# One transformer layer on one core: where the sums of three groups per pair of heads are added up, and where their row sums stand on TensorE

## The reference, cut to what matters

```python
def _L0_attn_ref(hidden_states, w_qkv, w_o):          # S = 2048 tokens, 16 heads of 32
    q, k, v = ...                                      # projections of the normalised x
    scores = jnp.einsum('bhqd,bhkd->bhqk', q, k) * scale
    scores = jnp.where(causal, scores, jnp.finfo(scores.dtype).min)
    probs = jax.nn.softmax(scores, axis=-1)
    attn = jnp.einsum('bhqk,bhkd->bhqd', probs, v)
    return jnp.einsum('bsh,oh->bso', attn, w_o)
...
    xn = _layernorm(x, axis=-1)
    x = x + _L0_attn_ref(xn, ...) + _L0_ffn_ref(xn, ...)   # the second is a gated MLP, 512 -> 4096 -> 512
```

## Time and profile before

| what | value |
|---|---|
| median of 3 runs | 1793.34 us (1793.21 to 1793.80) |
| the profiled execution's own time | 1794.05 us |
| its span | 1792.1 us |
| TensorE busy | 1753.0 us, 98% |
| VectorE busy | 1236.9 us, 69% |
| GpSimd busy | 752.8 us, 42% |
| ScalarE busy | 708.7 us, 40% |

### The profile page before, as it was taken

The page is one execution under the profiler, slowest core; times in us unless marked ns, Lnnn a source line. Parts: engine busy times, 40 slices in busy tenths (PEclk is TensorE's granted clock), DMA queues, the critical chain, the costliest instruction groups (busy, mean ns, idle before and its releaser), DMA issues.

```text
span 1792.1 us, 28186 instructions
## 1 busy us (share of the span) xinstructions
PE 1753.0 (98%) x10112; PEld 1340.7 (75%) x10112; DVE 1236.9 (69%) x1834; ACT 708.7 (40%) x1107; POOL 752.8 (42%) x716
## 2 busy tenths in 40 slices
PE   7999999999999998999999999999999999999998
PEld 6887666566566555888888888888888888888887
DVE  5526888888888888786566567567567666656654
ACT  3323666666666674223232223233223223222322
POOL 1442888988988985022212221222222212222221
PEclk9999999999999999999999999999999999999999
DMA  8775054154054011600110110110110011010002
GB/s 284 221 231 157 11 105 88 25 106 89 24 105 90 23 45 55 202 22 23 35 35 0 35 35 0 35 35 0 35 35 21 14 35 30 5 35 0 1 0 95
DMA packets 75614, 108.55 MB, mean 61 GB/s; under 512 B 24912, under 2 KB 44992, under 8 KB 72384
## 3 DMA queue, kind: packets, MB, share of 16 engines
q1 hardware_dynamic: 75520, 107.34, 22.1%
HBM read 74.04 MB, written 29.59 MB: 58 GB/s over the span
## 4 chain that ended last, share of the span: by engine, by line
PE 60%; DVE 0%; ACT 0%; issue 0%; ACTq 0%
PE p_up L50 7%; PE p_v L50 7%; PE p_up L52 7%; PE p_v L51 7%; PE p_up L51 7%; PE p_v L52 7%; PE p_s L50 6%; PE p_s L52 6%; PE p_s L51 6%; PE p_s L340 0%; PE p_s L339 0%; PE p_s L345 0%; PE p_v L339 0%; PE p_v L340 0%; PE p_up L340 0%; PE p_up L339 0%
## 5 line engine op out<-in xcount | busy, mean ns | idle before, releaser
L1418 POOL TENSOR_SCALAR poly<-poly 128x1024 f32<-128x1024 f32 (+1 forms) x65 | 72.0, 1108 | 801.4 <-ACT poly L1375 801.4
L753 POOL TENSOR_TENSOR e_sum<-e_sb 128x512 f32<-128x512 f32 (+1 forms) x244 | 304.1, 1271 | 62.2 <-ACT e_sb L839 33.7
L922 DVE TENSOR_REDUCE max_part<-p_s 128x1 f32<-128x512 f32 x384 | 246.4, 681 | 56.8 <-PE p_s L1033 56.5
L839 ACT ACTIVATE e_sb<-p_v 128x512 f32<-128x512 f32 (+2 forms) x384 | 212.6, 603 | 115.8 <-PE p_v L1064 60.4
L1481 DVE SCALAR_TENSOR_TENSOR inter<-inter,gate 128x1024 f32<-128x1024 f32 (+1 forms) x65 | 78.6, 1209 | 241.1 <-ACT inter L1381 240.3
L50 PE MATMUL p_v<-xn_hi,w_hi 128*128 128x512 f32 x512 | 199.2, 389 | 0.0
L51 PE MATMUL p_v<-xn_lo,w_hi 128*128 128x512 f32 x512 | 199.2, 389 | 0.0
L52 PE MATMUL p_v<-xn_hi,w_lo 128*128 128x512 f32 x512 | 199.2, 389 | 0.0
L50 PE MATMUL p_up<-xn_hi,w_hi 128*128 128x512 f32 x512 | 199.2, 389 | 0.0
L51 PE MATMUL p_up<-xn_lo,w_hi 128*128 128x512 f32 x512 | 199.2, 389 | 0.0
L52 PE MATMUL p_up<-xn_hi,w_lo 128*128 128x512 f32 x512 | 199.2, 389 | 0.0
(11 more groups left out here) (190 smaller groups left out, 3469.4 us busy)
## 6 DMA issues: line engine op xcount, KB each, us to landing
k_stack<-qk_scratch SPq DMA_DIRECT2D x42, 256.0 KB, 8.0
qk_scratch<-out_hi SPq DMA_DIRECT2D x32, 256.0 KB, 2.6
qk_scratch<-out_lo SPq DMA_DIRECT2D x32, 256.0 KB, 3.3
q_stack<-qk_scratch SPq DMA_DIRECT2D x24, 256.0 KB, 6.5
xn_lo_scratch<-xn_lo SPq DMA_DIRECT2D x4, 1024.0 KB, 5.2
v_stack<-in_gate_up_s SPq DMA_DIRECT2D x64, 64.0 KB, 2.3
xn_lo<-xn_lo_scratch SPq DMA_DIRECT2D x4, 1024.0 KB, 13.1
scales<-in_gate_up_s SPq DMA_DIRECT2D x64, 64.0 KB, 2.4
```

The costliest lines, as they stand in the source:

```text
L753: nc.gpsimd.tensor_tensor(*operands(k, i), ALU.add).then_inc(pool_summed, 1)
L839: nc.scalar.activation(e_sb[:, first:first + len(heads), 0:w], scores_of(x), ACT.Exp, scale=SCALE).then_inc(exp_done, 1)
L922: nc.vector.reduce_max(part, p_s[:, slot[n] % S_BUFS, 0:w], AX.X).then_inc(maxed, 1)
L1418: nc.gpsimd.tensor_scalar(part_of(poly, h, parts), part_of(poly, h, parts), GELU_A, 1.0, ALU.mult, ALU.add).then_inc(poly_done, 1)
```

## The change

`join_sums` of a group k is moved, if the group after it is diagonal and has all its 8 units: from ahead of unit 7 of its own group to amid the units of the diagonal group, ahead of unit 3, or of unit 4 where a turn of maxima stands in that group. These are groups 1, 4 and 8 of pairs 0 to 6, 21 in all (the last is 68). On TensorE the `row_sums` of the group ahead of a diagonal one is moved behind the four `product_v` of the diagonal group. This holds for all 24 such groups, those of the last pair too, where `join_sums` stays where it was.

```diff
+            def join_late(k):
+                return k + 1 < NG and DIAG[GS * (k + 1) % NS] and len(units_of(k + 1)) == UNITS_GROUP
...
                 for n in units:
-                    if n == units[-1]:
+
+
+                    if k and join_late(k - 1) and n == units[S_BUFS if TURNS[k] else S_BUFS - 1]:
+                        join_sums(k - 1)
+                    if n == units[-1] and not join_late(k):
                         join_sums(k)
                     unit_max(n)
...
-                if k and not DIAG[GS * (k - 1) % NS]:
+                diag = DIAG[GS * k % NS]
+                if k and not DIAG[GS * (k - 1) % NS] and not diag:
                     row_sums(k - 1)
                 for g in range(GS * k, GS * k + GS):
                     product_v(g)
+                if k and not DIAG[GS * (k - 1) % NS] and diag:
+                    row_sums(k - 1)
                 if DIAG[GS * k % NS]:
                     row_sums(k)
                 some_units(7, 8)
```

## The result

The change makes the kernel a little slower. The median of 13 runs is 1796.97 us (1796.01 to 1798.53), that of the kernel before, run between them, 1792.81 us (13 runs, 1791.77 to 1794.44): a ratio of 1.0023 [1.0016, 1.003], which is 4.2 us [2.9, 5.4]. The forecast was 1794.7. The profiled execution took 1796.14 us, with a span of 1794.2; that of before took 1794.05 with a span of 1792.1. In two comparisons further down one execution was far slower than all others (2143.64 us of the kernel before, 7479.17 us of split_first): the ratios leave it out, and the medians, which hold it, move by 0.2 us at most.

What follows compares the result with a forecast made beforehand. TensorE, busy for 98% of the span, bounds the kernel; only its waits in the attention can be won. Seven pairs +1.05, multiplies in three +0.9, last pair -0.6: +1.35 on 1793.34 gives 1794.7 us, range 1787 to 1802.

Steps and rivals of the forecast that it cites:

- the likeliest case: No change that the measurement can tell, within 0.2% (3.6 us), held by the forecast and D; chance 0.43.
- Group 12, -0.25 us: Without additions ahead of unit 7, TensorE's two waits shrink and the late additions run undisturbed: -0.25 us a pair.
- Groups 13 and 14, +0.65: GpSimd, held 2.3 us, puts a long sum beside `join_sums` of group 13, then 3.0 us: +0.65 us a pair.
- group 15, 0: VectorE's 1.37 idle us take the late additions, 1.33 us with GpSimd held: 0 for TensorE.
- Groups 16 to 18, +0.3 (+0.6): Late GpSimd lengthens `join_sums` of group 16, group 17's shortens: +0.3 us net, +0.6 in pairs 2, 4 and 6.
- 19, -0.55: In group 19 maxima and turn come 0.6 us earlier without the additions ahead: -0.55 us a pair.
- The last pair, -0.6: Group 79's products fill TensorE's idle time, row sum 1.16 us earlier; half taken lest the clock rise no earlier: -0.6.
- The sign named: A pair of heads taking 0.15 us more bears out the sum, 0.8 less A, 1.3 more B.
- A: Rival: GpSimd takes up its delays at `join_sums` of groups 13 and 16, gains stand alone: -6.2, 1787.1 us; chance 0.27.
- B: Rival: delays land in full at `join_sums` of group 16, group 19 gains only 0.2: +8.5, 1801.8 us; chance 0.22.
- C: Rival: row sums wait for 3.2 us additions in groups 12 and 15, 0.2 in 19: +13.4, 1806.7 us; chance 0.08.
- D: Rival: nothing hangs on it, waits for maxima pass to ScalarE's pace and back: 1793.3 us; chance 0.43 with the forecast.

Runs made afterwards that it cites:

- split_first: The changed kernel with GpSimd's split of the maxima ahead of its first two sums in groups 3, 13, ...: 1796.15 us, 1.0015 of the kernel before.
- late_1: The changed kernel with `join_sums` late only for groups 1, 11, ... 61: 1803.05 us, 1.005 of the kernel before.
- hold_only: The kernel before with the row sums moved and GpSimd held in groups 2, 12, ... 62 until VectorE's fifth unit is done: 1804.39 us, ratio 1.006.
- late_4: The changed kernel with `join_sums` late only for groups 4, 14, ... 64: 1793.83 us, 1.0004 of the kernel before.
- norm_later: The changed kernel with GpSimd's multiply moved from behind group 4 to behind group 5 in pairs 2, 4, 6 and the last: 1798.94 us, 1.003 of before.
- late_8: The changed kernel with `join_sums` late only for groups 8, 18, ... 68: 1789.86 us, 0.9984 of the kernel before.
- recip_late: The changed kernel with VectorE's reciprocal for the pair before moved from the group's head to ahead of unit 3: 1796.14 us, 1.0016 of the kernel before.
- late8_rows_before: The kernel before with `join_sums` late only for groups 8, 18, ... 68, row sums still ahead of the products: 1795.0 us, ratio 1.0007.
- late8_both: As late_8, with the reciprocal ahead of unit 3 and the last pair's multiply behind group 75: 1787.76 us, 0.9968 of the kernel before.
- late8_norm7: As late_8, with GpSimd's multiply behind group 74 (last pair alone) moved behind group 75: 1789.39 us, 0.9978 of the kernel before.
- rows_only: The kernel before with only TensorE's row sums moved behind the products, `join_sums` at its old place: 1793.03 us, ratio 0.9997.

## Why the prediction was right, and where it was off

The time came out 2.3 us above the forecast and inside the range. The range stated for the likeliest case, within 0.2%, was missed by a hair: +0.23% [0.16, 0.3], a little slower and not level. The mechanism is the forecast's: the late additions hold GpSimd, and `join_sums` of group 13 pays for it. Several sizes in it were not right, and they erred both ways; that the sum of them came out within 2.3 us is in part luck.

- *Group 12, -0.25 us.* Measured -0.20 in groups 12, 32, 42 and 62, and -0.14 in 22; 0.00 in group 2, which has no reciprocal. Together 7 x 0.25 = 1.75 was forecast, and the trace has 0.23, as one wait for the reciprocal's transfer takes 0.95 back.
- *Groups 13 and 14, +0.65, and group 15, 0.* Measured +0.60 to +0.65 in pairs 0, 1, 3 and 5. `join_sums` of group 13 takes 2.87 us where 3.0 was said, and GpSimd is held 2.3 us as said. That this size came out right is luck: by late_1 and hold_only the hold alone costs 1.1, and moving the additions of group 14, put at 0, gives 0.5 back.
- *The same in pairs 2, 4 and 6.* Here the step failed. "I take +0.65 us" was used for all seven pairs, and for group 15 "0 for TensorE" on the ground that GpSimd is held there. In these pairs GpSimd, late from the hold, is at its multiply (338.79) when the late additions come, and these take 2.49 us; by late_4, split_first and norm_later it takes both, the hold and the multiply. Measured +1.31, +1.58 and +1.30: 2.2 us more than forecast in sum, the largest part of the miss.
- *Groups 16 to 18, +0.3 (+0.6), and 19, -0.55.* Measured together -0.49 to -0.52 in the plain pairs, where -0.25 was said, and +0.05 in pairs 4 and 6, as said. Group 19 was right: late_8 gives -0.56 to -0.61 by itself. The +0.3 wasn't there: the additions of group 16 take 2.68 us in place of 1.84, those of group 17 2.82 in place of 3.20, and by late_1 and late_4 nothing of GpSimd's lateness is left over in TensorE's time (-0.02 and +0.05).
- *The last pair, -0.6.* Measured -1.15 at the row sums, which was the lower bound. I took half, lest the clock rise later. It did rise later: 706 to 712 is at the lower level, where before it was on its way up from 708 on (below). But from the row sums to the end of the span there are 1085.2 us in the change and 1085.9 before; over all 14 traces it is 1085.2 to 1086.7, whichever order they have. Nothing that can be told from that scatter was given back.

```profile
706.00:708.00 2.00, 0.46 (x8) 0.20 (x8) 1.85 (x4) 0.00 (x0) 0.00 (x0) 0.50 0.42 112
708.00:710.00 2.00, 1.60 (x20) 0.65 (x12) 1.84 (x5) 0.00 (x0) 0.00 (x0) 0.50 0.23 75
710.00:712.00 2.00, 2.00 (x9) 1.58 (x6) 2.00 (x4) 0.00 (x0) 0.00 (x0) 0.53 0.00 0
```

(The windows above are the changed kernel's; these are the same of the kernel before, whose second row sum came 2.8 us earlier in its trace.)

```profile
708.00:710.00 2.00, 2.00 (x9) 1.27 (x6) 1.41 (x1) 0.00 (x0) 0.00 (x0) 0.73 0.03 8
710.00:712.00 2.00, 2.00 (x10) 1.66 (x9) 1.87 (x5) 0.13 (x1) 0.00 (x0) 1.00 0.00 0
```

- *The sum.* From +1.35 to the trace's +3.3: +2.2 from pairs 2, 4 and 6, +1.5 from group 12 (its transfer, and pair 0), -1.0 from groups 16 to 19, and -0.55 from the last pair come to +3.5; -0.1 in groups 13 to 15 of the plain pairs and -0.1 in the pieces that were not to change make up the rest. The 0.9 us between these 3.3 and the 4.2 of the runs stay open. The transfer of the reciprocal may wait more often in other executions, which no trace shows; recip_late, which has no such wait, lies 2.8 us above the kernel before in place of 4.2, but that is not clear of the noise.
- *By pairs.* The sign named was a pair of heads that takes 0.15 us more, 0.8 less for A, 1.3 more for B. From one group 9 to the group 9 of the next pair, pairs 1 and 3 took 0.1 us less, pair 5 took 0.8 more with its wait for the reciprocal's transfer, and pairs 2, 4 and 6 took 1.1 to 1.4 more (the clock of before taken out). So neither kind of pair has the forecast's number: the plain ones came out under it and the others near B's, by another path.
- *The rivals.* A (GpSimd takes up its delays) is refuted by the 2.87 us of group 13. B (they land in full, with the price in group 16) named the right sign and the wrong place: the price lies in groups 13 to 15. C is refuted: the change's row sums wait for additions once, in group 79. late8_rows_before shows the wait of C where the row sums keep their place. D (nothing hangs on it) is refuted by the interval of the ratio, which lies above 1.
- *What was missing.* That VectorE, with two additions fewer ahead of it, reaches the reciprocal before its data has landed. The order shown ahead of the prediction has that row with its wait for `sums_loaded`; I read it only as "the reciprocal follows".

## What to carry to other kernels

When work is moved later on an engine, ask who waits for what it frees: here the freed buffers held a third engine for 2.3 us, and that by itself cost 1.1 us in a plain pair and 1.8 or 1.9 in one with multiplies (2.9 to 3.3 where TensorE's clock fell too), a whole group further on, while the moved instructions themselves ran undisturbed in the plain pairs. Try the places of such a move one at a time: of three, each with the moved row sums, one gained 0.6 us a pair at next to no cost (3.4 us in the runs, the row sums' gain in the last group with it), one was neutral by itself, and one lost 9.8. And work out each pattern of groups by itself: a price taken from a plain pair was wrong by a factor of two in the pairs in which the same engine has more to do. Last, look at the clock in both traces before a difference between them is read: seven of the 14 traces here have a stretch at the lower level that the others don't, worth up to 1.7 us.

## What the runs showed of the hardware

- Two additions of VectorE on two SBUF inputs (128x512, float32) take 1.28 to 1.33 us with GpSimd still or at small pieces, and 2.49 to 3.43 beside GpSimd's sums and its multiply in the rows shown. Maxima of 128x512 in PSUM take 0.67 to 0.69 us in either case, all but a few. The Trainium skill ("SBUF — State Buffer", section "Who interferes with whom") says that a VectorE instruction with two SBUF inputs contends with a GpSimd instruction that reads SBUF and that `tensor_reduce` never does on trn2. The traces agree with the first; the second is not tested here, as these maxima read PSUM, but nothing in them speaks against it.
- GpSimd's busy time holds this waiting too. It fell from 752.8 to 739.5 us with the same 716 instructions: 60 of its sums overlap with additions of VectorE, where 85 did before. It says nothing of the kernel's time: it is 753.9 us in hold_only, the slowest kernel, and 746.2 in late_8, which is faster than the kernel before.
- TensorE stood 4.75 us ahead of the row sums of group 79 and had a granted clock of 0.50 from 706 to 710 us and 0.53 from 710 to 712, its lower level of 1.2 GHz, though it was at work from 707.54 on.
- A single profiled execution can hold a stretch at the lower clock that others don't have. That of before (0.91 over 20 us) was worth 1.05 us, a quarter of the timed difference; that of late8_both (0.50 from 657.2 to 660.4 us) 1.67. What TensorE did ahead of them differs: it had waited 0.47 us (late8_both), 0.7 (before, late8_rows_before), 1.2 (late8_norm7), 1.5 (late_1, hold_only) and 2.2 (norm_later), and rows_only has the same wait as before in that place and no lower clock.
